# Holding back the store of the gates and the first down weights until the first gathered rows are there

## The reference

```python
w = weights[conditions]                         # 32 of 200 matrices, 64 x 64
xf = einsum('bct,bcd->bdt', x, w)               # as 2048 rows of 512
gate = softmax(xf @ Wr.T); top2_val, top2_idx = top_k(gate, 2)
keep = rank_within_expert <= 640                # cap = 1.25 * 2048 * 2 / 8
g = silu(einsum('nh,eih->eni', xf, Wg)); u = einsum('nh,eih->eni', xf, Wu)    # I = 352
out_e = einsum('eni,ehi->enh', g * u, Wd)
y = einsum('ne,enh->nh', comb, out_e); return x + y
```

## Time and profile before

| | us |
|---|---|
| median of 3 runs (lowest, highest) | 274.97 (272.59, 279.91) |
| span of the profiled execution | 271.4 |
| PE, DVE, ACT, POOL busy in it | 256.5, 160.8, 137.6, 173.0 |

### The profile page before, as it was taken

One profiled execution on the slowest core, in us unless ns is written; L12 is line 12 of the kernel. 1 busy time (PEld: TensorE's weight loads), 2 busy tenths in 40 slices (PEclk: granted clock), 3 DMA queues, 4 the chain that ended last, 5 costly groups with the idle time before them and its releaser, 6 DMA issues.

```text
span 271.4 us, 3936 instructions
## 1 busy us (share of the span) xinstructions
PE 256.5 (95%) x1368; PEld 199.2 (73%) x1368; DVE 160.8 (59%) x329; ACT 137.6 (51%) x242; POOL 173.0 (64%) x156
## 2 busy tenths in 40 slices
PE   7899697999999999899999999999999999999992
PEld 3563165999987877688878887777687777878981
DVE  2558996444459672877466639674865777243251
ACT  2256843344464674374466654675465548552100
POOL 5791038741158877883788288868885885488472
PEclk9999979999999999999999999999999999999999
DMA  6995898989888999899789878999899899456462
GB/s 185 367 328 203 336 281 266 403 319 314 310 261 178 231 209 297 150 229 301 171 165 225 256 203 133 192 313 271 139 244 343 157 170 212 87 63 81 100 220 104
DMA packets 29867, 61.22 MB, mean 226 GB/s; under 512 B 7664, under 2 KB 7792, under 8 KB 29744
## 3 DMA queue, kind: packets, MB, share of 16 engines
q1 hardware_dynamic: 19184, 37.89, 44.4%
q0 software_dynamic: 10656, 22.98, 40.1%
HBM read 39.56 MB, written 20.25 MB: 220 GB/s over the span
## 4 chain that ended last, share of the span: by engine, by line
PE 52%; DVE 16%; DMA 15%; issue 7%; ACT 5%; POOL 1%; SPq 1%; POOLq 0%; ACTq 0%; DVEq 0%
PE bank L1327 14%; PE bank L1414 11%; PE bank L1301 10%; DMA xg<-xf_dram,src_turn 9%; PE bank L1422 6%; DVE w L990 5%; DVE squares L1039 5%; DMA x_sb<-x 3%; PE bank L1219 2%; PE bank L1288 2%; PE bank L1163 2%; ACT hhi L687 2%; DMA xg<-xf_dram,src_row 2%; DMA xf_dram<-xf_sb 1%; PE bank L1175 1%
## 5 line engine op out<-in xcount | busy, mean ns | idle before, releaser
L1414 PE MATMUL bank<-xhi,w 128*128 128x512 f32 x280 | 71.7, 398 | 2.3 <-DVE h_last L1085 2.3
L545 POOL DMA_INDIRECT out<-y_sb,dst_row x35 | 61.3, 1751 | 15.5 <-issue 10.1
L1327 PE MATMUL bank<-w,hhi 128*128 128x512 f32 (+1 forms) x216 | 67.0, 392 | 0.0
L1414 PEld LDWEIGHTS bank<-xhi,w 128*128 128x128 f32 x280 | 52.2, 188 | 16.0 <-DVE h_last L1085 3.8
L513 POOL DMA_INDIRECT gate_g<-gates_dram,src_row x40 | 45.2, 1130 | 12.0 <-issue 11.4
L990 DVE TENSOR_TENSOR w<-raw,w 128x704 fp32r<-128x704 f32 (+1 forms) x35 | 37.0, 1057 | 14.6 <-ACT w L600 8.2
L1327 PEld LDWEIGHTS bank<-w,hhi 128*128 128x128 f32 x216 | 39.3, 188 | 8.7 <-DVE hlo L1045 1.0
L1327 PE MATMUL bank<-w,hlo 128*128 128x512 f32 (+1 forms) x108 | 41.9, 388 | 0.0
L501 POOL DMA_INDIRECT xg<-xf_dram,src_turn x24 | 23.8, 990 | 27.3 <-DVE xlo L975 12.5
L1422 PE MATMUL bank<-xlo,w 128*128 128x512 f32 x140 | 38.4, 396 | 0.0
L600 ACT ACTIVATE w<-raw 128x704 fp32r<-128x704 f32 (+1 forms) x40 | 36.7, 922 | 0.0
(11 more groups left out here) (135 smaller groups left out, 301.7 us busy)
## 6 DMA issues: line engine op xcount, KB each, us to landing
raw<-wgu SPq DMA_DIRECT2D x32, 352.0 KB, 7.5
xg<-squares SPq DMA_DIRECT2D x24, 256.0 KB, 6.2
x_sb<-x SPq DMA_DIRECT2D x8, 512.0 KB, 7.9
raw<-wd SPq DMA_DIRECT2D x8, 512.0 KB
xf_dram<-xf_sb SPq DMA_DIRECT2D x7, 512.0 KB, 3.3
raw<-wd SPq DMA_DIRECT2D x8, 192.0 KB
out<-x SPq DMA_DIRECT2D x1, 1280.0 KB, 18.2
gate_g<-gates_dram,src_row POOLq DMA_INDIRECT x40, 6.3
```

Source lines behind the costliest of these rows:

```text
L545: nc.gpsimd.indirect_dma_start(out=out[:, :], in_=y_sb[:, n % TPE, :], in_offset=None, out_offset=bass.IndirectOffsetOnAxis(ap=dst_row[:, ...
L1327: last = nc.tensor.matmul(ps[:, cols], left(c), w[:, half, part, o:o + width], start=(c == 0 and q == 0), stop=(closes and c == cs[-1] and ...
L1414: last = nc.tensor.matmul(ACC_BANK[what][:, :], columns(what, k, part), xhi4[:, k, :], start=(k == 0 and part == 0), stop=False)
```

## The change

SP waits for the first gather before it stores the gates, and not after it has started the store and the load of expert 0's down weights. On ACT the high part of these weights is made in step 0 of expert 0, after the high part of the second tile and before the Silu of the first. On DVE the low part is made in step 0 after the product of gate and up of the first tile. No work is added or taken away.

```diff
@@ block.sync
+            sp.wait_ge(xg_in[0], 16)
             sp.wait_ge(gates_ok, 2)
             sp.dma_start(gates_dram..., gate[:, :, :]).then_inc(gates_out, 16)
             load_unit(0, KH)
-            sp.wait_ge(xg_in[0], 16)
             for u in range(NU):
                 sp.wait_ge(wlo0_ok, u + 1)
                 load_unit(1, u)
@@ ACT first_expert
                     x_high(s + 1)
+                if s == 0:
+                    w_high(KH, 0, 0)
                 act.wait_ge(gu_ps, s + 1)
                 nc.scalar.activation(g_sb..., ACT.Silu).then_inc(silu_ok, n)
@@ ACT
             x_high(0)
-            w_high(KH, 0, 0)
@@ DVE first_expert
                 token_product(gate_up_banks(s)[1]).then_inc(h_ok, n)
+                if s == 0:
+                    w0_low(KH)
@@ DVE
             x_low(0)
-            w0_low(KH)
```

## The result

The changed kernel takes 279.1 us (median of 4 runs, 276.43 to 281.18) against 275.59 for the kernel before in the same comparison (272.59 to 279.91): ratio 1.014, 95% interval 1.0072 to 1.0208. The ratio leaves out slow executions, over 1.5% above the fastest of their kernel, and so is not the quotient of the medians. It is slower; whether by more than 2% the interval leaves open. The prediction was 276.9 and slower by 1.9; its range of 273.0 to 281.0 holds the time. The profiled execution has a span of 274.7 against 271.4, 3.3 more.

A forecast was written before the change was run, and what follows sets the result against it. The prediction saw a chain of waits through the first gather, then almost PE alone. Gather gain -0.1, stall +1.8 and what queues behind +0.2 made +1.9: span 273.3, median 276.9 us, range 273.0 to 281.0.

The forecast's parts named there:

- Part 1: First gather of rows without the gates' and down weights' traffic: gain of 0.1 us taken, bounds 0 and 0.89.
- the 2.52 against 2.35: Time behind POOL's instruction, first gather against a later one of the same size: transfer can win 0.17 at most.
- the 0.08 behind their end: POOL's first gather part ends 0.08 behind DVE's low parts of units 1 to 3; read as POOL waiting for DVE.
- Part 2: Down weights of expert 0 land later, holding up ACT's Silu: PE stall of 1.8 us, bounds 0 and 3.8.
- T0: The moment the first gather of rows lands, 42.43 in the kernel before; PE has nothing to do until then.
- the third of the four in the row: Third of SP's four 352 KB loads, landing 6.3 after issue (49.6); taken for the down weights' landing, as 49.7.
- the second load's row: Second of SP's four 352 KB loads, landing 4.9 after issue (47.8); down weights landing then would cost no stall.
- The clock: TensorE's clock behind PE's stall: a fall losing 1.4 to 2 appeared only in a rival, at 1.7.
- Part 3: What queues behind: gates, expert 1 loads and gathers, copies to the output; 0.2 us taken, from 0 to 1.2.
- the copies slip: Rival: stall of 3.8, late output copies cost 1.2 at expert 1's turns, clock 1.7; +6.6, 281.6 us; chance 0.14.
- the cover holds: Rival: weights land by 47.9, Silu isn't late, only the gather's 0.1 gain is left; 274.9 us; chance 0.22.
- it works as it is built: Rival: gather gains up to 0.89, POOL held by descriptors' traffic and not DVE, no stall; 274.1 us; chance 0.12.

The follow-up runs named there:

- e2: Kernel before, with only the down weights' high part (ACT) and low part (DVE) moved to the change's new places, SP as before; one run 277.16 us.
- e6: Kernel before, with DVE's 16 small copies for src_turn put ahead of the low parts of units 1 to 3; ratio 1.0017.
- e4: Kernel before, with only the store of the gates waiting for the first gather; down weights loaded and split at the old places; ratio 1.0103.
- e3: Changed kernel, with the gates stored ahead of the wait for the first gather and only the down weights held back; ratio 1.0043.
- e8: Changed kernel, with the down weights' high part moved behind tile 0's hidden rows on ACT and their low part likewise on DVE; ratio 1.0089.
- e1: Kernel before, with SP's part of the change alone; ACT and DVE split the down weights at the old places; one run 282.87 us.
- e5: Changed kernel, with 12 extra matmuls, results overwritten, right before PE waits for the first hidden rows; ratio 1.0124.
- e9: Changed kernel, with the down weights loaded ahead of the gates behind the wait for the first gather; one run 280.42 us.
- e11: Kernel before, with down weights loaded near 18 us, DVE's copies after one low part, gates behind the wait, two expert 1 gathers sent earlier; ratio 0.9978.
- e12: Kernel before, with down weights loaded near 18 us and DVE's copies after one low part; gates' store and POOL's list as before; ratio 1.001.

## Why the prediction was right, and where its terms were off

The direction and the place were right, and of the mechanism the main part: the weights that land too late hold up the Silu on ACT, and PE waits before it turns the hidden rows. Of its terms, four were off, and the errors cancel in part: 0.8 too little gain at the gather against 1.1 too little stall and 1.6 of clock left out.

**Part 1, the gain at the gather: 0.1 taken, 0.93 measured** from list to landing (42.43 - 36.55 = 5.88 before, 41.31 - 36.36 = 4.95 after): 0.83 in the gather itself (4.18 to 3.35), near the upper bound of 0.89, and 0.10 by its earlier start. The step that failed is the conclusion from "the change leaves DVE's work on units 1 to 3 where it is", that POOL's part stays near 1.66. DVE's work did stay (its low parts begin 0.80 behind the list in both), but the gather's start didn't, and POOL's part fell to 1.01. All profiles side by side, landing read as the start of SP's next transfer (0.02 behind it):

| kernel | in the queues beside the gather | POOL's part | start to landing |
|---|---|---|---|
| before, e2 | gates, weights | 1.66, 1.65 | 4.20, 4.15 |
| e6 | gates, weights | 1.01 | 4.45 |
| e4 | weights | 1.49 | 3.87 |
| e3, e8 | gates; nothing | 1.67, 1.71 | 4.00, 4.01 |
| after, e1, e5, e9, e11 | nothing | 1.01 to 1.07 | 3.35 to 3.46 |
| e12 | gates | 1.01 | 3.38 |

The landing is long when POOL's part is long or when the weights are beside it, and short only when both are gone. Taking one away alone brings 0.2 or nothing, which is what the 2.52 against 2.35 had shown for the weights; taking both away brings 0.8. The gates don't count here. POOL's part is decided by DVE: in e6 the low parts alone were moved, and it fell to 1.01. In the changed kernel they stayed, but the gather began 0.80 behind their start and not 0.90 (37.96 less 37.16; 38.25 less 37.35). Each piece takes some 0.83, so POOL met the end of the first piece and not the beginning of the second. It waits for the piece that it meets, and not for all three, as the 0.08 behind their end was read: counted from the start of the low parts, POOL ends at 2.56 to 2.58 in the kernel before, e2, e3, e4 and e8, and at 1.76 to 1.81 in the changed kernel, e1, e5 and e9, one piece less.

The start of the gather moved with what released it. Before, the last thing that POOL waited for was the landing of the last store of `xf_dram` (37.50, first row below); in the changed kernel, where nothing followed that store in the queues, it was DVE's list (37.26, second row):

```profile
33.74 3.76 DMA xf_dram<-xf_sb
```

```profile
37.05 0.21 DVE dst_row L951
```

But a tenth of a us decides it. e8, with the same list on SP, was released by the store all the same, started 0.86 behind the low parts and took 1.71; the changed kernel, e1, e5 and e9 started 0.69 to 0.80 behind. So what POOL wins here is in part luck.

By the working of the prediction the weights would cost nearly nothing if the queues share, and 1.9 if they are served in order; e6 against e12, where POOL's part is 1.01 in both, shows 1.07, between the two. The Trainium skill (DMA: Bandwidth & Descriptors, queues, rings and completion order) has each DMA engine go round robin between the queues; in these runs that doesn't make the weights free. The Trainium skill (SBUF — State Buffer, who interferes with whom) infers that VectorE instructions with two SBUF inputs leave descriptor making alone, but has them hold up a GpSimd instruction that reads SBUF. The gather's instruction reads its list of rows there, so these runs show that POOL waits, and leave open for which of the two.

**Part 2, the stall: 1.8 taken, 2.94 measured.** The weights were to land at T0 + 7.3; they came 8.4 behind, and these 1.1 are the whole difference. Most of it is SP: I let the last load go out 0.9 behind T0, as the third of the four in the row did, but behind the gates the first load's issue took 1.14, and the second began 1.59 behind T0. The row for this was there: before, the first load behind the gates took 1.71 to issue; with no gates ahead it takes 0.38 (e3, e9) or 0.64 (e4). The rest is the way, 6.8 and not 6.4.

e3 (6.85) shows the store of the gates as the cause of 1.59 of the 8.44: not 2, and 1.2 of it before the data move, in SP's issue. e9 (5.9) lands another 0.95 sooner, near the 5.4 of the second load's row. There the gathers of the gates aren't beside the weights either: POOL sends them from 49.44 on, against 45.25 in e3. How much of the 0.95 is theirs isn't shown. The low part of unit 4 at its new place cost nothing, as said (e2).

**The clock: 0 in the forecast, 1.61 measured.** The three pieces behind the idle stretch took (0.90 - 0.33) + (0.85 - 0.44) + (2.58 - 1.95) more, at a granted clock of 0.58 over 52 to 56, near the lower of the two levels; e5 gives 1.47 of it back. The prediction had this in the rival of the slipping copies, at 1.7, but tied it to a stall of 3.8, and put nothing for it into its own sum.

**Part 3: 0.2 taken, 0 measured.** The copies did start at 54.98, as forecast (55.0), and the turns for expert 1 didn't wait. Their first gather got ahead of the copies (52.64, 6.6 to land), and the fourth, which the prediction named, took 16.0 from 61.67 to 77.7, 2.4 before PE wanted it at about 80. That this was a near thing e3, e4 and e9 show: 0.34, 1.62 and 3.83 lost there. In e3 it was the fourth gather, as the rival *the copies slip* has it. In e4 and e9 it was the first, behind the copies by 2.66 and 3.76. So the mechanism of the rival is real, but it has a second trigger that the prediction hadn't: not copies that move late, but gathers that come behind them.

Together -0.93 + 2.94 + 1.61 = 3.62, against 3.66 in the stage. Of the other rivals, *the cover holds* and *it works as it is built* fell with the 2.94, though the second had the size of the gain at the gather right, for another reason. Of the signs, the idle time of PE and the start of the copies came as said; POOL's part did not, and the Silu came 3.7 later relative to T0 and not 2 to 3 (51.16 - 41.31 against 48.56 - 42.43). Not settled: why SP's first load needed 1.14 in the changed kernel and 2.17 in e8.

## What to carry to other kernels

Two things that delay the same transfer needn't add: here what counted was the later of them, so the price of taking away one was found only with the other gone. A transfer that is held back to clear the way for another pays its issue time on the queue, its whole way, and whatever small-piece transfer stands before it. Moving it earlier into an idle stretch, as e11 and e12 do, avoided that and shortened the stage by 0.5 and 0.65, which the time of whole executions doesn't show. Where a long copy is queued, see which short gathers get in before it: the first gather for expert 1 took 3.3 to 8.5 ahead of the copies (after, e1, e3, e5, e8, e11), and 12.8 to 18.6 behind their start (before, e2, e4, e6, e9, e12).

## What the runs showed of the hardware

- In these runs POOL's indirect DMA waits for a low part of DVE (an instruction with two SBUF inputs) that began before it. In the changed kernel the gather at 52.64 took 2.07 and ended 0.83 behind the low part that had begun at 52.13 (52.13 + 1.75 = 53.88); unhindered it is 0.95.
- In the stage TensorE's clock fell behind idle stretches of 2.94 (after), 4.59 (e1) and 3.83 (e9), and not behind 1.34 (e3), 1.62 (e4) and 2.32 (e8). The length of the last idle stretch alone doesn't decide: elsewhere it fell behind 1.50 (every kernel, before the products for the lists), 1.76 (e4, 0.57 in 199 to 203 us) and 2.00 (e3, 0.57 in 226 to 230), and stayed at 1.00 behind 1.99 (e11, 196 to 200).
- Such falls later in the program go with longer times. From the first product of expert 1 to the end, the six profiles without one there (the last slice left out) take 192.2 to 194.8, the six with one 194.1 to 198.2. How much of the spread between executions this is, one profile for each kernel doesn't show, and the waits ahead of the falls cost time as well. e2 has the same stage as the kernel before, yet takes 196.7 from there to the end against 192.4. Its busy time by stretch has the granted clock at 0.50 behind a stretch in which PE worked 1.02 of 4 us:

```profile
100.00:104.00 4.00, 1.02 (x5) 0.49 (x3) 0.94 (x2) 1.54 (x3) 2.04 (x3) 0.91 0.88 254
104.00:108.00 4.00, 3.65 (x9) 2.92 (x10) 0.44 (x1) 1.45 (x3) 2.56 (x2) 0.50 0.83 307
```
